# Moving every second PSUM evacuation of a linear-recurrence kernel from ScalarE to VectorE

## The chip, the cores and the metric

The kernel runs on all 8 cores of one Trainium2 chip. Each core computes one of the eight batch entries on its own, and no core waits for another. The time is the device time in microseconds (us) of the slowest core. Engine names are those of the profile: PE is TensorE (PEld its weight loads), DVE is VectorE, ACT is ScalarE, POOL is GpSimd, SP is SyncE. Times in ns are marked.

## What is computed

The input x has 8 batch entries of 8192 time steps with 1024 features. The reference, cut to what matters:

```python
lam = sigmoid(log_lambda_raw)
values = (1.0 - lam) * (x @ Wb.T + bb)
h = linear_recurrence(lam, values)        # h[t] = lam * h[t-1] + values[t]
z = layernorm(h @ Wc.T + bc + x) * gamma + beta
x = layernorm(x + z)
# int8 product: rows of x and columns of rhs scaled by their absolute maximum / 127 and rounded
q_x, s_x = quantise(x, per row);  q_r, s_r = quantise(rhs, per column)
x = layernorm(x + (q_x @ q_r) * s_x * s_r)
```

## The kernel before, in words

**Tiling.** A core walks its 8192 time steps in 32 chunks of 256 (CT). A chunk has two row blocks of 128 time steps (i = 0, 1), and the 1024 features are eight blocks of 128 (j = 0 to 7). Three products run on PE:
- mm1 (line 515, `mm1_group`): values, feature-major. For each j one group of 24 matmuls with 256 columns: eight each for high x high, low x high and high x low halves of a bf16 split. Group j goes to PSUM bank psm1[j % 2].
- mm2 (line 393, `mm2_group`): the product with Wc, four groups of 24 matmuls with 512 columns.
- mm3 (line 429, `mm3_group`): the quantised product, four groups of 8 matmuls with 512 columns, evacuated by ACT in line 438.

**Evacuation and scan.** `v_evac(c, j)` (line 527) takes group j out of PSUM and applies scale 1 - lam and a bias, per partition: one ACT instruction of 128x256. `scan_j(c, j)` (line 541) then runs the recurrence over these 256 time steps in place, on DVE. When all eight scans are done, `h_split` casts h to bf16 on ACT (line 552) and POOL computes the remainder (line 554). mm2 needs both.

**The rest of a chunk.** `p1a_i`, `p1b_i` and `p2_i` are the first two LayerNorms and the quantising, for row block i: squares with accumulation on ACT (568, 600), small statistics on DVE (462, 464, 472) and ACT (466, 469), normalising on ACT (580, 606), gamma, beta and the sum with x on DVE (584, 587, 591), the absolute maximum on DVE (610), scaling on ACT (619), rounding on DVE (622). `ln3a_i` (479) and `ln3b_i` (491) are the last LayerNorm, of the chunk before.

**Order of the work.** The program is written out in rounds k = 0 to 33. Round k holds transposes and mm1 of chunk k, mm2 and the first two LayerNorms of chunk k-1, and mm3 and the last LayerNorm of chunk k-2. Each engine executes its steps in program order. In the second half of a round the eight pairs of a group of mm1 and its evacuation are spread between the LayerNorm parts:

```python
mm1_pair(0); p1b_i(k-1, 0); mm1_pair(1); ln3a_i(k-2, 0); mm1_pair(2); p2_i(k-1, 0)
mm1_pair(3); ln3a_i(k-2, 1); mm1_pair(4); p1b_i(k-1, 1); mm1_pair(5); ln3b_i(k-2, 0), ln3b_i(k-2, 1)
mm1_pair(6); p2_i(k-1, 1); y_store; x_load; mm1_pair(7); scan_j(k, 7); h_split(k)
```

`mm1_pair(j)` records group j, evacuation j and, from j = 1, scan j-1, in this order.

**Who waits for whom.** `Planner.step` derives the waits from names of tiles that are read and written. All eight evacuations and scans of a chunk use one name, `vh0` or `vh1`. So scan j-1 also waits for evacuation j, which stands ahead of it, and evacuation j waits for scan j-2. Group j of mm1 waits for evacuation j-2, since it writes the same bank of psm1.

Of the kernel before, what the change touches and what calls it, by code (L numbers as in the profile page):

```python
# [7 lines left out]
AF = mybir.ActivationFunctionType  # L8
OP = mybir.AluOpType
# [108 lines left out]
def build_nc(T=8192, CT=256):  # L118
# [17 lines left out]
    with contextlib.ExitStack() as stk:  # L136
        E = stk.enter_context

        def sbt(name, shape, dt=F32):
            return E(nc.sbuf_tensor(name, shape, dt))  # L140
# [11 lines left out]
        omlc = sbt("omlc", [128, NDT])  # L152
        omlbb = sbt("omlbb", [128, NDT])
# [37 lines left out]
        vh = [big1[:, 4096:6144], big1[:, 6144:8192]]  # L191
# [10 lines left out]
        psm1 = [E(nc.psum_tensor(f"psm1{i}", [128, 512], F32)) for i in range(2)]  # L202
# [7 lines left out]
        for en in ("sync", "gpsimd"):  # L210
            for r in range(Planner.NDMA):
                sems[f"{en}_dma{r}"] = E(nc.semaphore(f"s_{en}_dma{r}"))

        P = Planner()
# [3 lines left out]
               writes=["iotaA"])  # L218
        P.step("gpsimd", lambda e: e.iota(iotaB[:], [[0, 128]], channel_multiplier=1,
                                          allow_small_or_imprecise_dtypes=True),  # L220
               writes=["iotaB"])
        P.step("vector", lambda e: e.tensor_tensor(idf[:], iotaA[:], iotaB[:], OP.is_equal),
               reads=["iotaA", "iotaB"], writes=["idf"])
# [6 lines left out]
               reads=["wSc"], writes=["wSc"])  # L230
        P.step("vector", lambda e: e.reciprocal(i127[:], i127[:]), reads=["i127"], writes=["i127"])
        P.step("vector", lambda e: e.tensor_scalar(wNc[:], wSc[:], -1.0, 1.0, OP.mult, OP.add),
               reads=["wSc"], writes=["wNc"])
        P.step("vector", lambda e: e.tensor_scalar(cxc[:], wSc[:], C52, C23, OP.mult, OP.bypass),
               reads=["wSc"], writes=["cxc"])
        P.step("vector", lambda e: e.scalar_tensor_tensor(cxc[:], wNc[:], C23, cxc[:], OP.mult, OP.add),
               reads=["wNc", "cxc"], writes=["cxc"])
# [15 lines left out]
               reads=["lamc"], writes=["lamc"])  # L253
        P.step("vector", lambda e: e.tensor_scalar(omlc[:], lamc[:], -1.0, -1.0,
                                                   OP.mult, OP.subtract),
               reads=["lamc"], writes=["omlc"])
        P.step("vector", lambda e: e.tensor_tensor(omlbb[:], omlc[:], bbcol[:], OP.mult),
               reads=["omlc", "bbcol"], writes=["omlbb"])
# [19 lines left out]
        for jj in range(NDT):  # L278
            bk = jj % 2
            for kk in range(NDT):  # L280
# [3 lines left out]
                    reads=["wst", "idf"], writes=[f"pstx{bk}"])  # L284
                if kk % 4 == 3:
# [3 lines left out]
                        reads=[f"pstx{bk}"], writes=[f"rtst{jj}"])  # L289
        for jj in range(NDT):  # L290
# [5 lines left out]
               reads=["csc", "i127"], writes=["csc"])  # L296
        P.step("vector", lambda e: e.tensor_copy(icsc[:], csc[:]), reads=["csc"], writes=["icsc"])
        P.step("vector", lambda e: e.reciprocal(icsc[:], icsc[:]), reads=["icsc"], writes=["icsc"])
        for jj in range(NDT):
# [3 lines left out]
                reads=[f"rtst{jj}", "icsc", "zcol"], writes=[f"rtst{jj}"])  # L303
            P.step("vector", lambda e, s=sl: e.tensor_scalar(
                rtst[:, s], rtst[:, s], cxc[:], cxc[:], OP.add, OP.subtract),
                reads=[f"rtst{jj}", "cxc"], writes=[f"rtst{jj}"])
            P.step("vector", lambda e, s=sl: e.tensor_scalar(
                qrsT[:, s], rtst[:, s], 127.0, -127.0, OP.min, OP.max),
                reads=[f"rtst{jj}"], writes=["qrsT"])
        for jj in range(NDT):  # L310
            for kk in range(NDT):
# [3 lines left out]
                    reads=["qrsT", "idb"], writes=["pstq"])  # L315
            P.step("scalar", lambda e, j=jj: e.copy(qrs[:, j * D:(j + 1) * D], pstq[:]),
                   reads=["pstq"], writes=["qrs"])
# [5 lines left out]
            reads=["csrowd"], writes=["csbc"], dma=True)  # L323
# [200 lines left out]
        def v_evac(c, j):  # L524
            p = c & 1
            bk = j % 2
            P.step("scalar", lambda e, jj=j, b=bk, pp=p: e.activation(  # L527
                vh[pp][:, jj * CT:(jj + 1) * CT], psm1[b][:, 0:CT], AF.Identity,
                bias=omlbb[:, jj:jj + 1], scale=omlc[:, jj:jj + 1]),
                reads=[f"psm1{bk}", "omlbb", "omlc"], writes=[f"vh{p}"])  # L530

        def scan_j(c, j):
            p = c & 1
# [92 lines left out]
        for k in range(NCH + 2):  # L626
# [27 lines left out]
            def mm1_pair(j):  # L654
                if k < NCH:
                    mm1_group(k, j)
                    v_evac(k, j)
                    if j >= 1:
                        scan_j(k, j - 1)
# [79 lines left out]
```

How the kernel before makes its waits and increments, by code:

```python
    def replay(self, eng_name, e, sems):  # L105
        for waits, fn, dma, tag in self.steps[eng_name]:
            for sem_name, val in waits:
                e.wait_ge(sems[sem_name], val)
            if isinstance(fn, list):
                for f in fn[:-1]:
                    f(e)
                ins = fn[-1](e)
            else:
                ins = fn(e)
            ins.then_inc(sems[tag[0]], 16 if dma else 1)
# [581 lines left out]
            @blk.gpsimd  # L697
            def _(e):
                P.replay("gpsimd", e, sems)
                for r in range(Planner.NDMA):
                    uses = (n_out_dma - 1 - r) // Planner.NDMA + 1 if r < n_out_dma else 0
                    if uses > 0:
                        e.wait_ge(sems[f"gpsimd_dma{r}"], 16 * uses)
```

## Time and profile before

| | |
|---|---|
| median of 3 runs | 2704.59 us (2702.23 to 2815.58) |
| the profiled execution | 2701.14 us |
| span of its slowest core, core 1 | 2699.6 us (the cores: 2694.2 to 2699.6) |
| mean granted clock of TensorE on core 1 | 0.876 of full speed |
| busy: PE, DVE, ACT, POOL | 71%, 36%, 40%, 17% of the span |
| evacuation, line 527 (ACT, 256 times) | 551 ns each |
| scan, line 541 (DVE, 256 times) | 746 ns each |

The span reaches from the first to the last instruction of a core, and 1.5 us of the profiled execution's time lie around it. Busy is the time in which an engine executes, so the rest of its span is waiting. A granted clock of 1.0 is 2.4 GHz and one of 0.5 is 1.2 GHz.

### The profile page before, as it was taken

How to read it: one execution, taken by the hardware profiler on the slowest of the kernel's cores; microseconds unless marked ns; L12 is line 12 of the kernel's file. 1: busy time of each engine (PE TensorE's matmuls, PEld its weight loads, DVE VectorE, ACT ScalarE, POOL GpSimd, SP SyncE). 2: the span in 40 equal slices, each digit the busy share in tenths (PEclk: the TensorE clock that was granted, in tenths of full speed). 3: DMA queues.
4: the chain of work that ended last, by engine and by line, in shares of the span. 5: the costliest groups of instructions: out<-in, count | busy, mean ns of one | idle time of the engine just before them, and what ended most of it. 6: DMA issues, size and time to landing. Idle time of an engine off the chain costs nothing.

```text
span 2699.6 us, 32538 instructions; the slowest of 8 cores (2694.2 to 2699.6 us)
## 1 busy us (share of the span) xinstructions
PE 1912.0 (71%) x11392; PEld 1193.4 (44%) x11392; DVE 961.4 (36%) x1962; ACT 1068.6 (40%) x1733; POOL 456.1 (17%) x200
## 2 busy tenths in 40 slices
PE   0348777777777777777877777778777777778761
PEld 0125444444454444444544444445444444445430
DVE  1223333344333334343333333433333333433332
ACT  2133344444343444444433344443334444434333
POOL 0001121211112221120212211211122121112220
PEclk9999988888998888888989888889888888899885
DMA  5110000111101010000000000000011110100000
GB/s 148 62 39 1 17 32 32 32 32 32 32 1 32 32 32 32 32 32 32 13 19 32 32 32 32 32 32 28 5 32 32 32 32 32 32 32 1 31 16 31
DMA packets 23376, 83.88 MB, mean 31 GB/s; under 512 B 3248, under 2 KB 3248, under 8 KB 23216
## 3 DMA queue, kind: packets, MB, share of 16 engines
q1 hardware_dynamic: 14336, 47.72, 6.5%
q0 software_dynamic: 8880, 34.08, 3.1%
q8 instruction: 93, 1.52, 0.2%
q14 instruction: 67, 0.55, 0.1%
HBM read 48.24 MB, written 33.56 MB: 30 GB/s over the span
## 4 chain that ended last, share of the span: by engine, by line
PE 40%; ACT 21%; DVE 19%; issue 13%; POOL 3%; DMA 2%; DVEq 1%; ACTq 0%; SPq 0%; POOLq 0%
PE psm L393 25%; PE psm L429 8%; DVE big L541 4%; ACT big L606 3%; ACT big L619 3%; DVE stats L610 3%; DVE big L587 3%; DVE big L584 3%; POOL Ab L446 3%; ACT big L580 3%; ACT big L600 2%; ACT big L527 2%; PE pstq L369 2%; PE pstx L350 2%; ACT stats L466 2%
## 5 line engine op out<-in xcount | busy, mean ns | idle before, releaser
L515 PE MATMUL psm<-big,wbh 128*128 128x256 bf16 x4096 | 565.6, 291 | 269.9 <-ACT big L527 267.6
L515 PEld LDWEIGHTS psm<-big,wbh 128*128 128x128 bf16 x4096 | 420.2, 104 | 371.7 <-issue 293.9
L393 PE MATMUL psm<-wch,big 128*128 128x512 bf16 x2048 | 504.0, 391 | 0.4 <-POOL big L554 0.3
L438 ACT ACTIVATE Ab<-psm,zcol,stats 128x512 f32<-128x512 f32 x128 | 99.0, 774 | 598.2 <-PE psm L429 594.0
L393 PEld LDWEIGHTS psm<-wch,big 128*128 128x128 bf16 x2048 | 205.6, 101 | 249.8 <-issue 27.1
L515 PE MATMUL psm<-big,wbl 128*128 128x256 bf16 x2048 | 303.9, 298 | 0.0
L446 POOL TENSOR_TENSOR Ab<-Ab,csbc 128x1024 f32<-128x1024 f32 x64 | 150.4, 2350 | 731.1 <-ACT Ab L438 731.1
L409 DVE SCALAR_TENSOR_TENSOR big<-psm,big 128x512 f32<-128x512 f32 x128 | 88.5, 692 | 484.6 <-PE psm L393 481.3
L429 PE MATMUL psm<-qrs,big 128*128 128x512 bf16 x1024 | 244.2, 382 | 6.0 <-ACT Ab L438 5.2
L393 PE MATMUL psm<-wcl,big 128*128 128x512 bf16 x1024 | 242.1, 379 | 0.0
L515 PEld LDWEIGHTS psm<-big,wbl 128*128 128x128 bf16 x2048 | 219.3, 107 | 42.9
L369 PE MATMUL pstq<-idb,big 128*128 128x128 bf16 x512 | 74.2, 298 | 216.2 <-DVE big L622 105.8
L350 PE MATMUL pstx<-idf,big 128*128 128x128 f32 x512 | 128.2, 401 | 131.5 <-DMA big<-x 124.7
L541 DVE TENSOR_TENSOR_SCAN big<-lamc,big 128x256 f32<-128x256 f32 x256 | 191.1, 746 | 68.1 <-ACT big L527 64.8
L554 POOL TENSOR_TENSOR big<-big 128x2048 bf16<-128x2048 f32 x32 | 129.9, 4059 | 464.3 <-ACT big L552 464.3
L450 DVE SCALAR_TENSOR_TENSOR Ab<-Ab,big 128x1024 f32<-128x1024 f32 x64 | 78.4, 1226 | 296.1 <-POOL Ab L446 296.1
L568 ACT ACTIVATE big<-big 128x1024 f32<-128x1024 f32 x64 | 67.6, 1057 | 271.4 <-DVE stats L566 271.4
L527 ACT ACTIVATE big<-psm,omlbb,omlc 128x256 f32<-128x256 f32 x256 | 141.2, 551 | 84.1 <-PE psm L515 61.6
L499 POOL DMA_DIRECT2D y<-big x32 | 24.4, 762 | 882.1 <-ACT big L491 567.9
L358 DVE TENSOR_TENSOR big<-pstx,big 128x512 bf16<-128x512 f32 x128 | 88.4, 691 | 206.8 <-ACT big L355 170.1
L369 PEld LDWEIGHTS pstq<-idb,big 128*128 128x128 bf16 x512 | 44.3, 126 | 260.6 <-issue 260.5
L429 PEld LDWEIGHTS psm<-qrs,big 128*128 128x128 bf16 x1024 | 100.3, 98 | 129.0 <-issue 10.1
(72 smaller groups left out, 1794.2 us busy)
## 6 DMA issues: line engine op xcount, KB each, us to landing
big<-x SPq DMA_DIRECT2D x32, 1024.0 KB, 6.4
y<-big POOLq DMA_DIRECT2D x32, 1024.0 KB, 8.0
big<-wbT SPq DMA_DIRECT2D x1, 4096.0 KB, 23.5
big<-wcT SPq DMA_DIRECT2D x1, 4096.0 KB, 16.5
big<-rhs SPq DMA_DIRECT2D x1, 4096.0 KB, 15.8
gbc<-gamma SPq DMA_DIRECT2D x1, 512.0 KB, 7.3
bbc<-beta SPq DMA_DIRECT2D x1, 512.0 KB, 8.3
ccbc<-bc SPq DMA_DIRECT2D x1, 512.0 KB, 11.1
```

The costliest lines, as they stand in the source:

```text
L350: items.append((lambda e, j=jj, i=ii, oo=o, b=bk, pp=p: e.transpose(pstx[b][:, oo * 128:(oo + 1) * 128], x_[pp][:, i * D + j * 128: i * D ...
L358: P.step("vector", lambda e, gg=g, b=bk, pp=p: e.tensor_tensor(xl[pp][:, 2 * gg * CT: 2 * (gg + 1) * CT], pstx[b][:, 0:512], xh[pp][:, 2 * ...
L369: items.append((lambda e, j=jj, i=ii, oo=o, pp=p: e.transpose(pstq[:, oo * 128:(oo + 1) * 128], q_[pp][:, i * D + j * 128: i * D + (j + 1) ...
L393: e.matmul(psm2[b][:, 0:512], hh[pp][:, kk * CT + ii * 128: kk * CT + (ii + 1) * 128], ww[:, kk * D + nn * 512: kk * D + (nn + 1) * 512], ...
L409: acc=sc("szn", i * 2 + n, 1): e.scalar_tensor_tensor(B_[pp][:, ii * D + nn * 512: ii * D + (nn + 1) * 512], psm2[b][:, 0:512], 1.0, A_[pp ...
L429: st=(k == 0), sp=(k == NDT - 1): e.matmul(psm3[:, 0:512], qT[pp][:, kk * CT + ii * 128: kk * CT + (ii + 1) * 128], qrs[:, kk * D + nn * 5 ...
L438: e.activation(Ab[:, ii * D + nn * 512: ii * D + (nn + 1) * 512], psm3[:, 0:512], AF.Identity, bias=zcol[:], scale=s),
L446: P.step("gpsimd", lambda e, ii=i: e.tensor_tensor(Ab[:, ii * D:(ii + 1) * D], Ab[:, ii * D:(ii + 1) * D], csbc[:], OP.mult), reads=["Ab", ...
L515: st=(idx == 0), sp=(idx == nmm - 1): e.matmul(psm1[b][:, 0:CT], w[:, kk * D + jj * 128: kk * D + (jj + 1) * 128], xx[pp][:, kk * CT:(kk + ...
L527: P.step("scalar", lambda e, jj=j, b=bk, pp=p: e.activation(vh[pp][:, jj * CT:(jj + 1) * CT], psm1[b][:, 0:CT], AF.Identity, bias=omlbb[:, ...
L541: P.step("vector", lambda e, jj=j, pp=p, ini=init: e.tensor_tensor_scan(vh[pp][:, jj * CT:(jj + 1) * CT], lamc[:, jj:jj + 1].broadcast_to( ...
L554: P.step("gpsimd", lambda e, pp=p: e.tensor_tensor(xl[pp][:], vh[pp][:], xh[pp][:], OP.subtract), reads=[vhk, xhk], writes=[xlk])
```

## The change

`v_evac` keeps its ACT instruction for even j. For odd j (1, 3, 5, 7) the same evacuation is a `tensor_scalar` on DVE, with the same scale and bias as two pointer scalars (one value per partition each). Names of tiles read and written stay the same, and so does the place in the program. All lines behind it have a number that is higher by 6, so the scan becomes line 547, line 591 becomes 597, line 622 becomes 628.

```diff
         def v_evac(c, j):
             p = c & 1
             bk = j % 2
-            P.step("scalar", lambda e, jj=j, b=bk, pp=p: e.activation(
-                vh[pp][:, jj * CT:(jj + 1) * CT], psm1[b][:, 0:CT], AF.Identity,
-                bias=omlbb[:, jj:jj + 1], scale=omlc[:, jj:jj + 1]),
-                reads=[f"psm1{bk}", "omlbb", "omlc"], writes=[f"vh{p}"])
+            if j % 2 == 0:
+                P.step("scalar", lambda e, jj=j, b=bk, pp=p: e.activation(
+                    vh[pp][:, jj * CT:(jj + 1) * CT], psm1[b][:, 0:CT], AF.Identity,
+                    bias=omlbb[:, jj:jj + 1], scale=omlc[:, jj:jj + 1]),
+                    reads=[f"psm1{bk}", "omlbb", "omlc"], writes=[f"vh{p}"])
+            else:
+                P.step("vector", lambda e, jj=j, b=bk, pp=p: e.tensor_scalar(
+                    vh[pp][:, jj * CT:(jj + 1) * CT], psm1[b][:, 0:CT],
+                    omlc[:, jj:jj + 1], omlbb[:, jj:jj + 1], OP.mult, OP.add),
+                    reads=[f"psm1{bk}", "omlbb", "omlc"], writes=[f"vh{p}"])
```

DVE's queue in a round of the middle, before, from the beta addition of row block 0 to the maximum of p2 (in these lists `big` stands for any of the large working tiles, `psm` for the PSUM banks of the products, and the scan is printed as SCALAR_TENSOR_TENSOR with lamc):

```order
L587 TENSOR_TENSOR big<-big,bbc 128x1024
L591 SCALAR_TENSOR_TENSOR big,stats<-big 128x1024
L541 SCALAR_TENSOR_TENSOR big<-lamc,big 128x256
L462 TENSOR_TENSOR stats<-stats 128x1
L464 SCALAR_TENSOR_TENSOR stats<-stats 128x1
L472 SCALAR_TENSOR_TENSOR stats<-stats 128x1
L541 SCALAR_TENSOR_TENSOR big<-lamc,big 128x256
```

The same stretch of DVE's queue in the changed kernel:

```order
L593 TENSOR_TENSOR big<-big,bbc 128x1024
L597 SCALAR_TENSOR_TENSOR big,stats<-big 128x1024
L533 TENSOR_SCALAR big<-psm,omlc,omlbb 128x256
L547 SCALAR_TENSOR_TENSOR big<-lamc,big 128x256
L462 TENSOR_TENSOR stats<-stats 128x1
L464 SCALAR_TENSOR_TENSOR stats<-stats 128x1
L472 SCALAR_TENSOR_TENSOR stats<-stats 128x1
L547 SCALAR_TENSOR_TENSOR big<-lamc,big 128x256
```

Evacuation 1 (line 533) stands between the sum with x and scan 0. Evacuation 5 stands in the same way behind the second line 597 of the round.

DVE's queue at the end of a round, before, from the reciprocal of row block 1 on (the rounding, the last two scans, the x transposes' remainders):

```order
L616 RECIPROCAL stats<-stats 128x1
L622 TENSOR_SCALAR big<-big,cxc 128x1024
L541 SCALAR_TENSOR_TENSOR big<-lamc,big 128x256 x2
L358 TENSOR_TENSOR big<-pstx,big 128x512 x4
L409 SCALAR_TENSOR_TENSOR big,stats<-psm,big 128x512 x2
```

The same in the changed kernel:

```order
L622 RECIPROCAL stats<-stats 128x1
L628 TENSOR_SCALAR big<-big,cxc 128x1024
L533 TENSOR_SCALAR big<-psm,omlc,omlbb 128x256
L547 SCALAR_TENSOR_TENSOR big<-lamc,big 128x256 x2
L358 TENSOR_TENSOR big<-pstx,big 128x512 x4
L409 SCALAR_TENSOR_TENSOR big,stats<-psm,big 128x512 x2
```

Evacuation 7 stands between the rounding and scans 6 and 7. Evacuation 3 stands behind the first rounding of the round, ahead of scan 2.

ACT's queue in the same round, before, from the scaling of row block 0 (line 619) to evacuation 6:

```order
L619 ACTIVATE big<-big,zcol,stats 128x1024
L527 ACTIVATE big<-psm,omlbb,omlc 128x256
L479 ACTIVATE big,stats<-Ab 128x1024
L466 ACTIVATE stats<-stats,epscol 128x1
L469 ACTIVATE stats<-stats 128x1
L527 ACTIVATE big<-psm,omlbb,omlc 128x256
L580 ACTIVATE big<-big,stats 128x1024
L527 ACTIVATE big<-psm,omlbb,omlc 128x256
L491 ACTIVATE big<-Ab,stats 128x1024 x2
L527 ACTIVATE big<-psm,omlbb,omlc 128x256
```

And in the changed kernel:

```order
L625 ACTIVATE big<-big,zcol,stats 128x1024
L479 ACTIVATE big,stats<-Ab 128x1024
L466 ACTIVATE stats<-stats,epscol 128x1
L469 ACTIVATE stats<-stats 128x1
L528 ACTIVATE big<-psm,omlbb,omlc 128x256
L586 ACTIVATE big<-big,stats 128x1024
L491 ACTIVATE big<-Ab,stats 128x1024 x2
L528 ACTIVATE big<-psm,omlbb,omlc 128x256
```

Evacuations 3 and 5 are gone from it, and 4 and 6 (line 528) remain. PE's queue is the same in both kernels.

## Rows read from the trace of the kernel before

**Rows 1.** The page, part 1: busy us, share of the span and instructions.

```profile
PE 1912.0 (71%) x11392; PEld 1193.4 (44%) x11392; DVE 961.4 (36%) x1962; ACT 1068.6 (40%) x1733; POOL 456.1 (17%) x200
```

**Rows 2.** The waits: engine, line, waited for, us in total, times, longest.

```profile
PE psm L515 <- ACT big L527: 267.6, 91, 5.2
```

**Rows 3.** The chain of waits, 1286 to 1372 us: start, us, what.

```profile
1345.51 0.68 DVE big L541
```

**Rows 4.** Timeline, place 1: start, us, engine, line, operation, count, idle before.

```profile
1327.61 0.08 DVE L591 DVE_READ_ACCUMULATOR big<-big 128x1 f32 x1
1327.61 0.74 DVE L541 TENSOR_TENSOR_SCAN big<-lamc,big 128x256 f32<-128x256 f32 x1
1328.27 0.13 DVE L462 TENSOR_TENSOR stats<-stats 128x1 f32<-128x1 f32 x1
1328.76 0.29 ACT L466 ACTIVATE stats<-stats,epscol 128x1 f32<-128x1 f32 x1 [3.57 <-DVE stats L464]
```

**Rows 5.** Timeline, place 3.

```profile
1337.14 0.54 ACT L527 ACTIVATE big<-psm,omlbb,omlc 128x256 f32<-128x256 f32 x1
1337.34 0.81 DVE L622 TENSOR_SCALAR big<-big,cxc 128x1024 bf16<-128x1024 f32 x1 [1.44 <-ACT big L619]
1337.59 1.04 ACT L479 ACTIVATE big<-Ab 128x1024 f32<-128x1024 f32 x1
...
1337.94 1.87 PE L515 MATMUL psm<-big,wbh 128*128 128x256 bf16 x8 [5.10 <-ACT big L527]
1338.07 0.75 DVE L541 TENSOR_TENSOR_SCAN big<-lamc,big 128x256 f32<-128x256 f32 x1
1338.54 0.19 ACT L479 ACTIVATION_READ_ACCUMULATOR big<-Ab 128x1 f32 x1
1338.83 0.16 DVE L462 TENSOR_TENSOR stats<-stats 128x1 f32<-128x1 f32 x1
```

**Rows 6.** Timeline, place 5: in the round before, and in this one.

```profile
1269.00 0.75 DVE L541 TENSOR_TENSOR_SCAN big<-lamc,big 128x256 f32<-128x256 f32 x1
...
1269.87 0.55 ACT L527 ACTIVATE big<-psm,omlbb,omlc 128x256 f32<-128x256 f32 x1
...
1343.24 2.56 ACT L491 ACTIVATE big<-Ab,stats 128x1024 f32<-128x1024 f32 x2
...
1345.43 0.08 DVE L591 DVE_READ_ACCUMULATOR big<-big 128x1 f32 x1
1345.43 0.75 DVE L541 TENSOR_TENSOR_SCAN big<-lamc,big 128x256 f32<-128x256 f32 x1
...
1346.27 0.56 ACT L527 ACTIVATE big<-psm,omlbb,omlc 128x256 f32<-128x256 f32 x1 [0.47 <-DVE big L541]
```

**Rows 7.** Timeline, place 7.

```profile
1353.90 0.55 ACT L527 ACTIVATE big<-psm,omlbb,omlc 128x256 f32<-128x256 f32 x1
1354.10 0.81 DVE L622 TENSOR_SCALAR big<-big,cxc 128x1024 bf16<-128x1024 f32 x1 [1.44 <-ACT big L619]
1354.83 1.60 DVE L541 TENSOR_TENSOR_SCAN big<-lamc,big 128x256 f32<-128x256 f32 x2
```

**Rows 8.** Groups of instructions by form: busy us, mean ns, idle before.

```profile
L527 ACT ACTIVATE big<-psm,omlbb,omlc 128x256 f32<-128x256 f32 x256 | 141.2, 551 | 84.1 <-PE psm L515 61.6 <-DVE big L541 17.8 <-DVE big L584 4.1
...
L409 DVE SCALAR_TENSOR_TENSOR big<-psm,big 128x512 f32<-128x512 f32 x128 | 88.5, 692 | 484.6 <-PE psm L393 481.3
...
L591 DVE SCALAR_TENSOR_TENSOR big<-big 128x1024 f32<-128x1024 f32 x64 | 78.4, 1225 | 7.0 <-DVE big L587 0.5
...
L304 DVE TENSOR_SCALAR big<-big,cxc 128x1024 f32<-128x1024 f32 x8 | 6.5, 807 | 1.4 <-ACT big L301 1.4
L307 DVE TENSOR_SCALAR big<-big 128x1024 bf16<-128x1024 f32 x8 | 5.5, 694 | 0.9
```

**Rows 9.** Timeline, PE in groups 5 to 7 of mm1, the round before.

```profile
1261.51 1.87 PE L515 MATMUL psm<-big,wbh 128*128 128x256 bf16 x8 [4.82 <-ACT big L527]
...
1263.17 1.91 PE L515 MATMUL psm<-big,wbl 128*128 128x256 bf16 x8
...
1268.43 1.91 PE L515 MATMUL psm<-big,wbh 128*128 128x256 bf16 x16
```

## The prediction

> **What bounds the kernel now.** I read the page first, then the waits, then the chain of work that ended last, and last the timeline of one round. On the page the reader sees that no engine is full: PE is busy 1912.0 us of 2699.6, DVE 961.4, ACT 1068.6 [rows 1]. Busy time therefore says nothing about who sets the end, and "ACT has more work than DVE, so move some over" is not an argument by itself. In the waits PE stands idle before a group of line 515 (the first product, mm1) for 267.6 us in 91 waits, each ended by an ACT instruction of line 527 [rows 2]. That invites a second error, that the evacuation of line 527 is slow. It takes 0.55 us [rows 8]. PE waits because line 527 stands in ACT's queue behind other work, and that work is a ping-pong between ACT and DVE: LayerNorm statistics, normalising, quantising, for two row blocks in turn.
>
> The chain shows which pieces count. In this half of a round it runs through the scans of line 541 on DVE [rows 3], and the timeline shows why at four places of a round:
> - Place 1, between lines 591 and 462: the scan starts as line 591's accumulator is read (1327.61), line 462 starts 0.66 later, and ACT, idle for 3.57 us, goes on with line 466 once line 464 is done [rows 4]. ACT has slack here, DVE none.
> - Place 3, behind the quantising of line 622: the scan starts 0.73 after line 622 and ends at 1338.82. ACT's line 479 ends with its accumulator at 1338.73, and line 462 starts at 1338.83 [rows 5]. Both sides arrive nearly together.
> - Place 5, behind the second line 591: scan 4 starts at 1345.43, and evacuation 6 on ACT starts 0.84 later, because the planner makes it wait for that scan. ACT had been idle for 0.47 us [rows 6]. One round earlier the distance is 0.87, with ACT just free (1269.00 to 1269.87), so in both rounds the scan is as late as anything.
> - Place 7, behind the second line 622: scans 6 and 7 start at 1354.83 and take 1.60; evacuation 7 on ACT (1353.90, 0.55 long) was over by 1354.45 [rows 7]. The cast of line 552, the rest of h_split, PE's transposes and the second product (mm2) all follow from scan 7.
>
> So from the first line 591 to the end of the round the path runs through DVE at exactly the four places where the odd evacuations will now stand. None of the four odd line 527s is on that path today.
>
> **The change part by part.** *Removed from ACT:* four evacuations a round, each 0.45 us from its start to the next instruction's (1337.14 to 1337.59 [rows 5]). Number 1 goes where ACT waits 3.57 us afterwards, so it is worth nothing. Number 3 goes ahead of line 479, which then ends 0.45 earlier, but line 462 also waits for the scan, so it is worth at most the 0.09 us between 1338.74 and 1338.83 (1338.74 is where line 462 would start 0.08 before the scan's end, as it does at place 1 [rows 4]). Number 5 stands ahead of the two line 491s (1343.24 plus 2.56, [rows 6]), after which ACT idles for the scan, worth nothing. Number 7 is hidden behind line 622, worth nothing. Together: 0.09 us a round.
>
> *Added on DVE:* four tensor_scalars from PSUM, 128x256 fp32, with two pointer scalars. No row of before shows this one, so I bound it. Line 409 is a DVE pass over 512 elements of PSUM in 692 ns, line 591 one over 1024 elements in 1225, so an element costs 533/512 = 1.04 ns, and 256 elements come to 692 - 266 = 426 ns [rows 8]. Two pointer scalars cost 807 - 694 = 113 ns, from the tensor_scalar with cxc twice (line 304) against the one with constants (line 307) [rows 8]. Sum: 0.54 us. Lines 304 and 307 do 1024 elements at half the price of an element. If that held from PSUM too, line 304's 807 less 768 elements at 0.52 gives 0.41 us, the low end. The high end is 0.75, the longest DVE pass of this size (the scan). I take 0.54, as line 409 is the row with the same source.
>
> On this the Trainium skill (VectorE: DVE Perf Modes, section "Why PSUM operands drop a tier") says that an fp32 operand in PSUM holds VectorE to one element a cycle. No row of a tensor_scalar from PSUM can confirm it here. By that rule the item is the 0.54; without it, 0.41. The same page (section on the TRN2 errata) gives 120 cycles plus the elements for VectorE from PSUM, an estimate of 376/0.96 = 392 ns; by it the sum below would be 4 x 0.49 - 0.09 = 1.87, times 31 = 58, and the time 2759. Line 409's 692 ns is above what that formula gives for 512 elements, 658, so here the trace says the page is low.
>
> Each added instruction also gets a gap behind it: the scan must wait for its result on the same engine, and two scans that do so take 1.60 for 2 x 0.75, a gap of 0.10 [rows 7]. So one place costs 0.64 us. In front there is no new gap, since the evacuation waits only for PE and for evacuations that are done, and can start where the scan starts now.
>
> *Along the path:* place 1 delays lines 462, 464 and ACT's 466 by 0.64. Place 3 delays line 462 by another 0.64 - 0.09. Place 5 delays scan 4 and thereby evacuation 6 and line 600 by 0.64. Place 7 delays scans 6 and 7 and the cast by 0.64. Queued behind each on DVE stands the statistics or scan chain, and ACT waits for exactly that. A round gets 4 x 0.64 - 0.09 = 2.47 us longer. Rounds k=1 to 31 have this shape (k=0 has no LayerNorm part, and its evacuations lie beside mm1; the last two have no mm1). 31 x 2.47 = 76.6 us.
>
> *PE:* bank 1 of psm1 now comes free when DVE gets there. PE starts 0.26 after an evacuation's end (1337.14 + 0.54, then 1337.94 [rows 5]). Group 3 of mm1 waits until 1327.61 + 0.54 + 0.26 = 1328.4. It is followed by group 4 and then by an idle PE anyway, so it costs nothing. Group 5 now follows evacuation 3 on DVE, at 1338.07 + 0.64 + 0.54 + 0.26 = 1339.5 instead of 1337.94 [rows 5], 1.57 later. Evacuation 6 needs group 6. In the round before, groups 5 and 6 ran from 1261.51 until about 1269.3 (the last eight of group 6 are the first half of the sixteen matmuls at 1268.43) [rows 9], 7.8 us; 1.57 later that is 1270.9. DVE allows evacuation 6 at 1269.87 + 3 x 0.64 - 0.09 = 1271.7. Covered by 0.8 us; if the cover goes, see the rival on PE. The x load is issued behind line 597, about 1.2 us later, and its transposes are not needed until the cast of h_split, which moves by more.
>
> *Sum:* the profiled execution took 2701.1 us, 3.5 below the median of 2704.6 of the runs. 2701.1 + 76.6 = 2777.7, that is 2778. With the low end of 0.41 us: 4 x 0.51 - 0.09 = 1.95, times 31 = 60, 2761. With the high end of 0.75: 3.31 x 31 = 103, 2804. A measurement of this kernel tells about 2% from no change, here 2759.
>
> **Rivals.**
> *Only half of the places count* (12%). If at place 3 the true last arrival is ACT's accumulator (1338.73 is within 0.1 us of the scan) and at place 5 it is ACT's own queue (as at 1269.87), ACT's relief of 0.45 pays back most of it. Then only places 1 and 7 cost: 1.28 x 31 = 40, 2741. Against it: at both places DVE was as late already, and there is no slack to take up 0.64.
> *ACT sets the round, and the change is a gain* (5%), the one that ends at not slower. This holds if the scans of places 1, 3, 5 and 7 had idle time of more than 0.64 ahead of their consumers; then the evacuations ahead of lines 479 and 491 leave the path, 2 x 0.45 x 31 = 28, 2673. It decides at place 3, by whether the scan's end was over 0.64 earlier than line 479's. For it speaks that ACT has 107 us more work than DVE [rows 1]; against it the times in rows 5 and 6.
> *PE becomes late* (8%). The half clock shows in group 5: eight matmuls take 1.66 us (1261.51 to 1263.17 [rows 9]), 0.21 each, the 1.2 GHz level, after PE had stood idle. If groups 5 and 6 both run so, that is 48 x 0.21 = 10.0 us instead of 7.8. Evacuation 6 comes at 1263.07 + 10.0 + 0.2 = 1273.3 instead of 1271.7, 1.6 more a round, 50 us in all, 2828. For it speaks that PE gets one more wait a round; against it that the clock was back before group 6 in that round although PE had stood still for almost 5 us. [...]
>
> **How the numbers follow.** The forecast, 2761 to 2804 with 2778 as its centre, has 70%, the rivals 12, 5 and 8, and 5% stay for the clock's phase at the start of mm2 and what I don't see. The range goes down to 2740, which takes in half of the first rival, and up to 2805. Outside lie the second rival, half of the first, most of the third. Slower by over 2%: 66 of the forecast's 70 (the rest is its cheap end), 8 of PE late, 4 of the remainder, 78%. Within 2%: 4, 12, 3 and 1, 20%. Faster by over 2%: 2%, if ACT's relief counted at all four places (56 us).
>
> **What would show it.** In the profile after: the new DVE group at about 540 ns, 128 times, DVE busy up by about 69 us and ACT busy down by about 70; scan 0 starting 0.64 after the accumulator read of line 597; evacuation 6 at 1.48 instead of 0.84 behind that read; ACT still idle ahead of line 466, by 0.64 plus 0.45 more; a new wait of PE for DVE ahead of groups 3, 5 and 7; the distance of one h_split cast to the next up by 2.5 us, and the mm2 stage unchanged. The forecast is wrong if line 462 at place 3 waits for ACT's line 479, if evacuation 6 waits for PE, or if the DVE evacuation takes under 0.4 us.

## The result, and the profile after

The changed kernel takes 2771.13 us, the kernel before 2703.59 us (medians of 8 runs each). The ratio of the two is 1.0251, with a 95% interval of 1.0240 to 1.0263, so the change makes the kernel 2.5% slower. The forecast was 2778, with a range of 2740 to 2805. In some executions of most kernels here the cores of one die show a lower granted clock and take longer (2815.58 us in one of the 8 before), and no comparison in this document uses them.

The profiled execution of the changed kernel took 2773.26 us. Its eight cores span from 2752.5 to 2771.7 us, while before they lay between 2694.2 and 2699.6. The page of the slowest, core 5, part 1 (answering to [rows 1]):

```profile
PE 1933.5 (70%) x11392; PEld 1203.9 (43%) x11392; DVE 1028.5 (37%) x2090; ACT 1010.4 (36%) x1605; POOL 456.0 (16%) x200
```

DVE has 67 us more work and ACT 58 us less. The forecast for ACT was 70, which counts the 0.55 us of each evacuation; an evacuation overlaps the next instruction on ACT, and 128 times the 0.45 us from its start to the next start are 58. By busy time the two engines are now balanced, and the kernel is slower. The reader should keep this row as the example of what busy time doesn't say.

The group of the new instruction, and the evacuation that stayed on ACT (by form: busy us, mean ns, idle before; answering to [rows 8]):

```profile
L528 ACT ACTIVATE big<-psm,omlbb,omlc 128x256 f32<-128x256 f32 x128 | 71.1, 555 | 123.3 <-DVE big L547 96.8 <-PE psm L515 26.4 <-issue 0.2
L533 DVE TENSOR_SCALAR big<-psm,omlc,omlbb 128x256 f32<-128x256 f32 x128 | 69.2, 541 | 12.3 <-PE psm L515 12.3
```

The new instruction takes 541 ns, not less than the 551 of the one it replaced. The waits (answering to [rows 2]):

```profile
ACT stats L466 <- DVE stats L464: 274.5, 191, 5.0
...
PE psm L515 <- DVE big L533: 221.8, 76, 5.8
...
ACT big L528 <- DVE big L547: 96.8, 32, 5.8
...
PE psm L515 <- ACT big L528: 83.9, 30, 3.1
```

PE's wait ahead of mm1 is now 221.8 + 83.9 = 305.7 us instead of 267.6. Most of it has changed its name, from ACT to DVE, and the whole has grown (core 5 here, core 1 there).

The timeline of core 5 at place 1, between the first sum with x and the statistics of ln3a (answering to [rows 4]):

```profile
1201.73 0.08 DVE L597 DVE_READ_ACCUMULATOR big<-big 128x1 f32 x1
1201.73 0.54 DVE L533 TENSOR_SCALAR big<-psm,omlc,omlbb 128x256 f32<-128x256 f32 x1
1202.37 0.75 DVE L547 TENSOR_TENSOR_SCAN big<-lamc,big 128x256 f32<-128x256 f32 x1
...
1203.04 0.13 DVE L462 TENSOR_TENSOR stats<-stats 128x1 f32<-128x1 f32 x1
...
1203.53 0.30 ACT L466 ACTIVATE stats<-stats,epscol 128x1 f32<-128x1 f32 x1 [4.67 <-DVE stats L464]
```

The scan starts 0.64 behind the accumulator read, where it used to start with it, and line 462 follows 1.31 behind it instead of 0.66. ACT idles 4.67 us instead of 3.57: the 0.64 by which DVE is later, and the 0.45 that ACT no longer spends on evacuation 1. ACT's relief has become ACT's idle time.

Place 3, behind the first rounding (answering to [rows 5]):

```profile
1212.03 1.04 ACT L479 ACTIVATE big<-Ab 128x1024 f32<-128x1024 f32 x1
1212.23 0.81 DVE L628 TENSOR_SCALAR big<-big,cxc 128x1024 bf16<-128x1024 f32 x1 [1.44 <-ACT big L625]
1212.96 0.54 DVE L533 TENSOR_SCALAR big<-psm,omlc,omlbb 128x256 f32<-128x256 f32 x1
1212.98 0.19 ACT L479 ACTIVATION_READ_ACCUMULATOR big<-Ab 128x1 f32 x1
1213.60 0.75 DVE L547 TENSOR_TENSOR_SCAN big<-lamc,big 128x256 f32<-128x256 f32 x1
1213.64 1.87 PE L515 MATMUL psm<-big,wbh 128*128 128x256 bf16 x8 [4.38 <-DVE big L533]
1214.27 0.13 DVE L462 TENSOR_TENSOR stats<-stats 128x1 f32<-128x1 f32 x1
```

ACT's line 479 is now done at 1213.17, over one microsecond ahead of line 462, which waits for the scan alone. PE starts group 5 at 1213.64, 0.14 after the end of evacuation 3.

Place 5, behind the second sum with x (answering to [rows 6]). Evacuation 6 on ACT starts 1.50 behind the accumulator read instead of 0.84, after 2.93 us of idle time. In all of the rounds 2 to 31 of this core it waits for the scan:

```profile
1220.85 0.08 DVE L597 DVE_READ_ACCUMULATOR big<-big 128x1 f32 x1
1220.85 0.54 DVE L533 TENSOR_SCALAR big<-psm,omlc,omlbb 128x256 f32<-128x256 f32 x1
...
1221.50 0.75 DVE L547 TENSOR_TENSOR_SCAN big<-lamc,big 128x256 f32<-128x256 f32 x1
1222.35 0.57 ACT L528 ACTIVATE big<-psm,omlbb,omlc 128x256 f32<-128x256 f32 x1 [2.93 <-DVE big L547]
```

The chain of work that ended last, in the same round, names evacuations on DVE as pieces of its own, at places 1, 3, 5 and 7 (start, us, what). Before, none of the odd ones was in it:

```profile
1201.81 0.47 DVE big L533
...
1212.96 0.55 DVE big L533
...
1220.94 0.47 DVE big L533
...
1230.91 0.55 DVE big L533
```

To see the whole kernel and not one round, I cut each of the rounds 2 to 31 of two cores at five marks of the timeline (starts of the first and second sum with x, of the first and second rounding, and of the cast of h) and took the median of each stretch, in us:

| stretch | before, core 0 | after, core 0 | after, core 5 | core 0 | forecast |
|---|---|---|---|---|---|
| first sum to first rounding (place 1) | 10.62 | 11.26 | 11.28 | +0.64 | +0.64 |
| first rounding to second sum (place 3) | 6.94 | 7.47 | 7.48 | +0.53 | +0.55 |
| second sum to second rounding (place 5) | 9.82 | 10.47 | 10.49 | +0.65 | +0.64 |
| second rounding to cast (place 7) | 2.42 | 3.07 | 3.06 | +0.65 | +0.64 |
| sum | 29.80 | 32.27 | 32.31 | +2.47 | +2.47 |

The rest of a round, from the cast over mm2 to the first sum with x, was forecast as unchanged. It isn't. Its mean over these 30 rounds falls from 46.76 to 46.22 us on core 0 and from 46.86 to 46.52 on core 5.

### The profile page after: what moved, and what is told of

Same layout as the page of the kernel before. It is cut to its first block, busy times and chain, and to the rows that moved or that the text cites. A ratio compares the mean times of both kernels' runs of the same rounds, so it can differ in the third digit from the quotient of the medians.

```text
span 2771.7 us, 32539 instructions; the slowest of 8 cores (2752.5 to 2771.7 us)
## 1 busy us (share of the span) xinstructions
PE 1933.5 (70%) x11392; PEld 1203.9 (43%) x11392; DVE 1028.5 (37%) x2090; ACT 1010.4 (36%) x1605; POOL 456.0 (16%) x200
## 4 chain that ended last, share of the span: by engine, by line
PE 39%; ACT 21%; DVE 19%; issue 15%; POOL 3%; DMA 2%; DVEq 1%; ACTq 0%; SPq 0%; POOLq 0%
PE psm L393 24%; PE psm L429 8%; ACT big L612 3%; ACT big L625 3%; DVE stats L616 3%; POOL Ab L446 3%; ACT big L586 3%; DVE big L593 3%; DVE big L590 3%; DVE big L547 3%; ACT big L606 2%; DVE big L533 2%; ACT big L528 2%; PE pstq L369 2%; PE pstx L350 2%
## 5 line engine op out<-in xcount | busy, mean ns | idle before, releaser
L515 PE MATMUL psm<-big,wbh 128*128 128x256 bf16 x4096 | 585.9, 297 | 307.9 <-DVE big L533 221.8
L515 PEld LDWEIGHTS psm<-big,wbh 128*128 128x128 bf16 x4096 | 426.8, 106 | 420.7 <-issue 335.4
L393 PE MATMUL psm<-wch,big 128*128 128x512 bf16 x2048 | 497.5, 387 | 0.4 <-POOL big L560 0.3
L515 PE MATMUL psm<-big,wbl 128*128 128x256 bf16 x2048 | 313.0, 304 | 0.0
L515 PEld LDWEIGHTS psm<-big,wbl 128*128 128x128 bf16 x2048 | 225.2, 110 | 48.2
L466 ACT ACTIVATE stats<-stats,epscol 128x1 f32<-128x1 f32 x192 | 57.1, 297 | 274.5 <-DVE stats L464 274.5
```

The costliest lines, as they stand in the source:

```text
L393: e.matmul(psm2[b][:, 0:512], hh[pp][:, kk * CT + ii * 128: kk * CT + (ii + 1) * 128], ww[:, kk * D + nn * 512: kk * D + (nn + 1) * 512], ...
L515: st=(idx == 0), sp=(idx == nmm - 1): e.matmul(psm1[b][:, 0:CT], w[:, kk * D + jj * 128: kk * D + (jj + 1) * 128], xx[pp][:, kk * CT:(kk + ...
```

## The experiments

### Single places

`only5` and `only7` move one evacuation each, all others stay on ACT.

```diff
-            if j % 2 == 0:
+            if j != 5:
```

> Only evacuation 5 on DVE, 1, 3 and 7 on ACT as before. Place theory (a DVE instruction put on the DVE part of the path costs its length and a gap): the stretch from the second sum with x to the second rounding grows by 0.65 us a round (9.82 to 10.47), the three other stretches stay, 31 x 0.65 = 20 us, ratio near 1.007, moved by up to 15 us by the clock at the start of mm2. Rival 'only half of the places count' (at place 5 ACT's own queue is the last arrival and its relief pays back): that stretch grows by 0.2 or less, 0 to 6 us.

> Only evacuation 7 on DVE, 1, 3 and 5 on ACT as before. Place theory: only the stretch from the second rounding to the cast of h grows, 2.42 to 3.07, 31 x 0.65 = 20 us, ratio near 1.007, moved by the clock. Rival: the cost is a matter of DVE's load, in which case all four stretches grow by a quarter of what the whole change gave each (0.16).

Measured: `only5` 1.0093 of the kernel before (95% interval 1.0050 to 1.0136), `only7` 1.0071 (1.0032 to 1.0111). Both intervals hold the 1.007 that was expected, and neither is narrow enough to give the price of one place, so the stretches decide. The stretches on core 0, medians: `only5` 10.62, 6.94, **10.47**, 2.42; `only7` 10.62, 6.94, 9.82, **3.06**. Place 5 of `only5`, on core 0:

```profile
1276.35 0.08 DVE L597 DVE_READ_ACCUMULATOR big<-big 128x1 f32 x1
1276.35 0.54 DVE L533 TENSOR_SCALAR big<-psm,omlc,omlbb 128x256 f32<-128x256 f32 x1
...
1276.99 0.75 DVE L547 TENSOR_TENSOR_SCAN big<-lamc,big 128x256 f32<-128x256 f32 x1
1277.84 0.56 ACT L528 ACTIVATE big<-psm,omlbb,omlc 128x256 f32<-128x256 f32 x1 [2.94 <-DVE big L547]
```

Each of the two evacuations costs 0.65 us a round in its own stretch and nothing in the other three. That refutes both rivals: the load theory would have spread the cost, and at place 5 ACT's relief pays nothing back. Each price is also the growth of the same stretch in the whole change, where the other three evacuations had moved as well. Evacuations 1 and 3 were not moved alone.

### ACT's relief taken back

`act_dummy` is the changed kernel plus an ACT instruction of the same size, on constant data into a scratch tile, at each place that an evacuation left.

```diff
+                P.step("scalar", lambda e, jj=j: e.activation(
+                    junk[:, 0:CT], ccbc[:, 0:CT], AF.Identity,
+                    bias=omlbb[:, jj:jj + 1], scale=omlc[:, jj:jj + 1]),
+                    reads=["ccbc", "omlbb", "omlc"], writes=["junk"])
```

> The changed kernel, and in addition an ACT instruction of the same size (128x256, from a constant tile into a scratch tile) at each place where an evacuation left ACT's queue, so ACT's relief is taken back and DVE's load stays. The added instruction is no part of the computation. Place theory: ACT's relief was worth nothing, so the four stretches stay within 0.05 us of the changed kernel's (11.26, 7.46, 10.47, 3.07) and the time within 0.5% of its 2771. Rival 'ACT's relief pays back part of the cost': 2 x 0.45 x 31 = 28 us more, 2799.

Measured: 2765.8 and 2776.6 us in two runs, on either side of 2771 and too few for an interval, so the rounds must decide. Their stretches on core 0 are 11.26, 7.46, 10.47 and 3.06, those of the changed kernel to 0.01, and the profiled cores span 2751.8 to 2775.0 us against its 2752.5 to 2771.7. Place 3 on core 5, with the added instruction in line 537 and the scan in line 551:

```profile
1288.65 0.58 ACT L537 ACTIVATE junk<-ccbc,omlbb,omlc 128x256 f32<-128x256 f32 x1
...
1290.08 0.19 ACT L479 ACTIVATION_READ_ACCUMULATOR big<-Ab 128x1 f32 x1
1290.22 0.75 DVE L551 TENSOR_TENSOR_SCAN big<-lamc,big 128x256 f32<-128x256 f32 x1
1290.89 0.13 DVE L462 TENSOR_TENSOR stats<-stats 128x1 f32<-128x1 f32 x1
...
1291.38 0.29 ACT L466 ACTIVATE stats<-stats,epscol 128x1 f32<-128x1 f32 x1 [1.11 <-DVE stats L464]
```

The only thing that moved is ACT's idle time, 1.11 us instead of 1.60 ahead of line 466. What the change took from ACT was worth nothing at all four places. That holds for place 3 too, whose stretch grows by 0.53 and not by 0.64: with the added instruction ACT's line 479 ends at 1290.27, still 0.62 ahead of line 462, and the stretch stays at 7.46. The missing 0.1 us is time that DVE had to spare there before, when line 462 waited for ACT.

### The shared names

`names` is the kernel before with a name for each block of `vh`, so the planner sets only waits that the data need. `names_dve` is the same edit on the changed kernel.

```diff
-                reads=[f"psm1{bk}", "omlbb", "omlc"], writes=[f"vh{p}"])
+                reads=[f"psm1{bk}", "omlbb", "omlc"], writes=[f"vh{p}{j}"])
...
-            vhk = f"vh{p}"
+            vhk = f"vh{p}{j}"
...
-            vhk = f"vh{p}"
+            vhk = [f"vh{p}{j}" for j in range(NDT)]
```

> The kernel before with all evacuations on ACT, but each of the eight blocks of vh has its own name in the planner, so that scan j-1 no longer waits for evacuation j and evacuation j no longer for scan j-2. Place theory: only place 5 gains, where evacuation 6 waited for scan 4 up to 0.47 us: the stretch from the second sum to the second rounding falls from 9.82 by 0 to 0.47, 0 to 15 us in all, ratio 0.995 to 1.0. Rival 'the shared names are what puts evacuation and scan on the path': about 0.5 us at each of four places, 60 us less, ratio 0.978.

> The changed kernel (odd evacuations on DVE) with a name of its own for each block of vh, as in the run 'names'. Place theory: against 'names' (10.62, 6.94, 8.96, 2.20 in the four stretches) places 1, 3 and 7 still cost, about 0.54 each since the scan behind the evacuation no longer waits for it (places 3 a little less), and place 5 costs nothing, since evacuation 6 on ACT no longer waits for scan 4: 11.1, 7.4, 9.0, 2.75, together 1.5 us a round. Rival 'the shared names made the DVE evacuation dear': all four stretches stay within 0.1 of those of 'names'.

Measured: `names` 0.9806 of the kernel before (0.9750 to 0.9862), faster, though not clearly by 2%; `names_dve` 1.0054 (1.0036 to 1.0071). The profiled execution of `names` spans 2656.4 us on its slowest core against 2699.6 before, 1.6% less. Stretches on core 5: `names` 10.62, 6.94, 8.96, 2.20; `names_dve` 11.07, 7.27, 9.47, 2.66. Place 5 of `names`, core 5:

```profile
1325.98 2.56 ACT L491 ACTIVATE big<-Ab,stats 128x1024 f32<-128x1024 f32 x2
...
1328.45 0.55 ACT L527 ACTIVATE big<-psm,omlbb,omlc 128x256 f32<-128x256 f32 x1
1328.46 0.08 DVE L591 DVE_READ_ACCUMULATOR big<-big 128x1 f32 x1
1328.46 1.39 DVE L541 TENSOR_TENSOR_SCAN big<-lamc,big 128x256 f32<-128x256 f32 x2
...
1328.90 1.05 ACT L600 ACTIVATE big<-big 128x1024 f32<-128x1024 f32 x1
```

Evacuation 6 now starts with the accumulator read and not 0.84 after it, and line 600 follows 0.44 behind that read. The place was named rightly, places 1 and 3 gained nothing, and so far this is the place theory. But both sizes were missed. The stretch fell by 0.86, not by 0.47 at most, for line 491 also started earlier than I had assumed (1.33 ahead of the second sum against 1.04). At place 7 the stretch fell by 0.22, which I had not forecast: two scans that don't wait for each other take 1.39 instead of 1.60 us. The ratio is near the one the rival named, yet not by its mechanism, which needed about 0.5 at each of four places. Averaged over 30 rounds of core 5 the four stretches fall by 0.97 us, which makes 29 us, and the part from the cast to the first sum falls from 46.86 to 46.29, another 17. The second part is the clock of the next section: 3 slow starts of mm2 instead of 15.

In `names_dve` the DVE evacuations cost, against `names`, 0.45 and 0.33 at places 1 and 3 and 0.46 at place 7, a little under the 0.54 of the instruction. So the rival falls: waits by name are not what makes the evacuation dear. At place 5, where I expected nothing, the cost is 0.51. The view of the waits on core 5 and the timeline of one round give the cause, `names_dve`:

```profile
ACT big L528 <- PE psm L515: 89.1, 36, 6.5
...
1345.49 1.86 PE L515 MATMUL psm<-big,wbh 128*128 128x256 bf16 x8 [3.57 <-DVE big L533]
...
1352.47 0.56 ACT L528 ACTIVATE big<-psm,omlbb,omlc 128x256 f32<-128x256 f32 x1 [1.41 <-PE psm L515]
```

In `names` this wait was 61.4 us in 41 times, and there all eight evacuations were on ACT. In `names_dve` the even ones alone wait 89.1: once evacuation 6 no longer waits for the scan it waits for group 6, which is late, because group 5 had to wait for evacuation 3 on DVE. Evacuation 6 waits for PE in all of the rounds 2 to 31, and in `names` in none of them. How late PE is goes along with its clock. In 10 of the 30 rounds the stretch is 9.01 us, 0.05 above the 8.96 of `names`, so there the expectation held, and the mean granted clock between evacuations 3 and 6 was 0.77 to 0.80. In the other 20 it is 9.24 to 10.64 us, at 0.64 to 0.78. That is the prediction's third rival, PE being late, in a kernel in which its cover of 0.8 us is gone.

### The clock at the start of mm2

The part of the round that got shorter holds mm2. PE's first eight matmuls of mm2 in three rounds running, kernel before, core 1:

```profile
1209.56 3.19 PE L393 MATMUL psm<-wch,big 128*128 128x512 bf16 x8
...
1286.75 2.15 PE L393 MATMUL psm<-wch,big 128*128 128x512 bf16 x8
...
1363.16 3.19 PE L393 MATMUL psm<-wch,big 128*128 128x512 bf16 x8
```

And of the changed kernel, core 4:

```profile
1310.01 1.89 PE L393 MATMUL psm<-wch,big 128*128 128x512 bf16 x8
...
1388.49 1.89 PE L393 MATMUL psm<-wch,big 128*128 128x512 bf16 x8
...
1466.96 1.89 PE L393 MATMUL psm<-wch,big 128*128 128x512 bf16 x8
```

Eight take 1.89 us at a granted clock of 1.00 (2.4 GHz), as in the last three rows, and 3.19 at a mean of 0.59, as in the first and the third. In both kernels PE does transposes before that, at 0.50 (1.2 GHz): before, 4.6 us of matmuls in the 9.5 us up to 1209.5. What differs is when the clock rises. In rounds 3 to 9 before, on core 1, that is in turn 2.0 to 2.4 us and 0.0 to 0.2 us behind the first matmul of mm2; after, on core 4, it is between 0.6 ahead and 0.7 behind in 16 of the rounds 2 to 19, and later in two. I call a start slow if the eight take over 2.3 us. In the rounds 2 to 31 there are 14 slow starts before on core 0 and 15 on core 5. After, it is 2 on core 0, none on core 1, 2 on core 4, 6 on core 7 and 9 on core 5. The stage itself has not changed. On core 5 the part from the cast to the first sum takes 46.10 us before and 46.15 after in rounds whose eight take at most 2.0 us, and 47.39 and 47.20 in rounds with a slow start. So the changed kernel loses less time to the clock, and cores lose differently, which is most of the 19 us by which their spans now differ: between core 6 and core 5 the 30 rounds make 14 us. The other 5 come ahead of the first cast, whose start differed between cores before as well (211.4 to 219.4 us). `pad7` adds one DVE instruction, on constant data, to ask whether the length of the round decides this.

```diff
+                if j == 7:
+                    P.step("vector", lambda e: e.tensor_tensor(
+                        junk[:, 0:512], ccbc[:, 0:512], csbc[:, 0:512], OP.add),
+                        reads=["ccbc", "csbc"], writes=["junk"])
```

> The changed kernel and one more DVE instruction ahead of evacuation 7 (128x512 from two constant tiles into a scratch tile, no part of the computation). Place theory: the stretch from the second rounding to the cast grows by 0.61 to 0.79 from 3.07, the others stay: 20 to 24 us. Clock theory (mm2's first matmuls are at half clock in about every second round of the kernel before and in hardly any of the changed kernel because the length of the round decides it): at 79.2 us a round they are at half clock again in a third to a half of the rounds, their eight take 2.5 us or more instead of 1.9, and the stretch from the start of mm2 to the last line 450 gets 0.3 to 0.6 longer: 30 to 42 us together, about 2805. Rival (the new waits ahead of mm2 keep the clock up): they stay at 1.9, 2793.

Measured: 2793.7 us, 1.0323 of the kernel before (1.0297 to 1.0349). Only the stretch of place 7 grew, 3.07 to 3.67. The first eight are slow in 9 rounds on core 0 and 12 on core 5, against 2 and 9. The die medians of the span went from 2757.1 and 2759.8 to 2786.0 and 2787.6, 28 to 29 us, of which 0.60 x 31 = 18.6 are the instruction. So slow starts did come back, as the clock theory said. But the whole time rose by 22.6 us, by which the rival's 2793 was right and my 2805 wrong: a whole time is that of the slowest core, and that core had 9 slow starts already. Length alone is not the rule either. `only5` and `only7`, at 77.3 to 77.5 us a round (medians), have 19 and 20 slow starts, each on both cores, `names_dve` at 77.3 only 9 on core 0 and 10 on core 5. That the clock gives back part of the cost is shown. What decides in which round stays open.

### The same instructions, in idle time

If place is all that counts, evacuations and scans should cost nothing where their engine waits anyway. `slots_act` has all evacuations on ACT, `slots_dve` the odd ones on DVE. Both have a name for each block of `vh`, as `names` has, and both record evacuations and scans in the idle times that the profile shows (core of `slots_act`, with `hook`, `slot_a` and `slot_b` called behind lines 464, 606 and 616):

```diff
+            def slot_a0():
+                ev(3); sn(2); mm(5); ev(4); mm(6)
+            def slot_b0():
+                sn(3)
+            def slot_a1():
+                ev(7); sn(6)
+            def slot_b1():
+                sn(7)
...
-            mm1_pair(1)
+            mm(1); ev(1); mm(2); mm(3)
             if 2 <= k:
-                ln3a_i(k - 2, 0)
+                ln3a_i(k - 2, 0, lambda: sn(0))
...
-                p2_i(k - 1, 0)
+                p2_i(k - 1, 0, slot_a0, slot_b0)
```

> All evacuations on ACT, own names, and evacuations and scans recorded where their engine is idle: evacuations 3, 4 and 7 behind the normalising of line 606, scans 0 and 4 behind line 464, scans 2 and 6 ahead of the maximum, 3 and 7 behind the reciprocal, 1 and 5 in the shadow of the squares. Place theory: place 1 gains 0.6, place 3 0.45, place 5 0.9, place 7 2.6 us a round (the cast then follows the scaling on ACT at once): 4.5 x 31 = 140 us less than before, 2560, moved by up to 20 by the clock. Rival (PE's product mm1 sets the round once the scans are out of the way): no stretch gains more than 'names' gave, 2655.

> The odd evacuations on DVE as in the changed kernel, but recorded like the scans where DVE is idle (1 behind line 464, 3 ahead of the first maximum, 5 behind the second sum, 7 behind the second reciprocal). Place theory: a DVE evacuation costs nothing where DVE waits anyway, so the time is within 1.5% of 'slots_act' and far below both kernels, 2560 to 2610. Rival 'an evacuation on DVE costs its length wherever it stands': 4 x 0.6 x 31 = 74 us above 'slots_act'.

Measured: `slots_act` 2539.64 us, 0.9381 of the kernel before (0.9356 to 0.9407), 6.2% faster. `slots_dve` took 2566.8 and 2567.5 us in two runs, too few for an interval, and its profiled execution's slowest core spans 2566.0 us against 2537.1 of `slots_act`, 1.1% more. The stretches on core 0, medians (in both kernels the cast starts ahead of the second rounding, so the last stretch is negative):

| stretch | before | slots_act | slots_dve |
|---|---|---|---|
| first sum to first rounding | 10.62 | 9.97 | 10.88 |
| first rounding to second sum | 6.94 | 6.03 | 6.04 |
| second sum to second rounding | 9.82 | 8.70 | 8.71 |
| second rounding to cast | 2.42 | -0.20 | -0.01 |
| sum | 29.80 | 24.51 | 25.61 |

The whole gain of `slots_act` is 5.29 us a round instead of the 4.5 expected: 0.65 and 2.62 at places 1 and 7 as expected, 0.91 and 1.12 at places 3 and 5 instead of 0.45 and 0.9. The names alone had given 0.86 and 0.22 of it, at places 5 and 7. Place 7 of `slots_act`, where the scan is line 543, the scaling 623, the rounding 626 and the cast 554:

```profile
1273.70 0.74 DVE L543 TENSOR_TENSOR_SCAN big<-lamc,big 128x256 f32<-128x256 f32 x1
...
1275.02 0.54 ACT L529 ACTIVATE big<-psm,omlbb,omlc 128x256 f32<-128x256 f32 x1
...
1277.03 0.75 DVE L543 TENSOR_TENSOR_SCAN big<-lamc,big 128x256 f32<-128x256 f32 x1
1277.19 1.24 ACT L623 ACTIVATE big<-big,zcol,stats 128x1024 f32<-128x1024 f32 x1 [1.62 <-DVE stats L619]
1278.33 1.88 ACT L554 CAST big<-big 128x2048 bf16<-128x2048 f32 x1
```

The cast follows the scaling at once, instead of waiting for the rounding and two scans. The rival that PE would set the round at 2655 is refuted.

Against `slots_act` the DVE evacuations cost 1.10 us a round, less than half of the 2.47 they cost in the changed kernel, and the rival's 74 us, which would be 2614, is too dear. The stretches show which of them cost. Evacuation 5 costs 0.01. Evacuation 7 costs 0.19: scan 7 now ends together with ACT's scaling (at 1356.59 and 1356.58 in one round), and the cast starts 0.10 behind it, where in `slots_act` it starts 0.10 ahead of the scaling's end. The other 0.91 lies in the first stretch, where evacuations 1 and 3 stand. One round of it on core 0, with the evacuation in line 535:

```profile
1333.33 1.87 PE L517 MATMUL psm<-big,wbh 128*128 128x256 bf16 x8 [3.08 <-DVE big L535]
...
1337.55 0.54 DVE L535 TENSOR_SCALAR big<-psm,omlc,omlbb 128x256 f32<-128x256 f32 x1 [1.21 <-PE psm L517]
```

Group 3 of mm1 waits for evacuation 1, which in its pause comes late, and evacuation 3 then waits for group 3, ahead of the maximum that the round needs. In 24 of the rounds 2 to 31 evacuation 3 waits 0.88 to 2.39 us for PE, at a mean granted clock of 0.50 to 0.68 from shortly before group 3 to evacuation 3, and the stretch is 10.77 to 12.43 us. In the other six the clock was 0.95 to 1.00, evacuation 3 doesn't wait, and the stretch is 9.97, that of `slots_act`. So the time of DVE in a pause costs nothing, as the place theory says. What it had left out is that a later evacuation also gives PE its bank later. Why the clock was up in those six rounds stays open.

## Why the prediction was right

The direction, the range and the mechanism held, and one term, the unchanged rest of a round, was wrong. Point by point:

- *The odd evacuations will stand on DVE's part of the path, at four places.* Right at each: four stretches grow, the chain names the four instructions, and those of places 5 and 7 have the same price alone (`only5`, `only7`).
- *The instruction takes 0.54 us.* 541 ns. It was worked out as one element in 1.04 ns, with the fixed part of line 409 and 113 ns for two pointer scalars. At half the price of an element it would have been 0.41. The Trainium skill's rule (VectorE: DVE Perf Modes, "Why PSUM operands drop a tier"), that an fp32 operand in PSUM holds VectorE to one element a cycle, agrees with the 541. The 392 ns that the prediction estimated from the same page's table for PSUM sources is too low.
- *A gap of 0.10 ahead of the dependent scan, 0.64 a place.* Right: 1201.73 to 1202.37.
- *ACT's relief is worth 0.09 us a round.* The 0.09 is right as a term, and the four stretches grew by the 2.47 of the sum, but it was put down to the wrong side. `act_dummy` takes the relief back and no stretch changes, so the relief is worth nothing. The 0.09 is what the scan of place 3 had to spare while line 462 waited for ACT.
- *PE is covered by 0.8 us.* Right for the changed kernel as far as evacuation 6 goes: it waits for the scan in all of the rounds 2 to 31. Group 5 started 0.14 behind the end of evacuation 3, not 0.26, and the size of the cover was not measured. In `names_dve`, whose evacuation 6 is no longer held by the scan, the late group 6 is the wait in all of them.
- *31 x 2.47 = 76.6 us, with the mm2 stage unchanged.* The unchanged stage is the term that was off. On core 0 the four stretches did give 2.48 (means), but the part from the cast to the first sum fell by 0.54 a round. 30 rounds of 1.93 and 2.6 in round 1 make 60.5, and the span grew by 58.9. On core 5, the slowest, 30 rounds of 2.19 and 3.8 in round 1 make 69.5; another 7.6 came ahead of the first cast, where the first cast starts at 219.0 instead of 211.4, a part that the edit hardly touches. Before, the eight cores' first casts lay between 211.4 and 219.4, so this is a difference between executions, and it happened to bring the time nearer to the forecast. The medians of the whole kernel differ by 67.5. I had put the clock's phase into the remainder with 5%, without a size or a sign. It was worth 10 us on core 5 and 16 on core 0, and it was a gain. Even so the range would have held: core 0 alone would have given about 2756.
- *The rivals.* Half of the places (2741), ACT sets the round (2673) and PE late (2828) did not happen. The first named places 3 and 5 as cheap. At place 5 the cost is full, 0.65, and at place 3 it is 0.53, which `act_dummy` leaves as it is.

## What to carry to other kernels

Before you move work to the less busy engine, find where it will stand in that engine's queue, and whether somebody waits for what is queued behind it. Here two engines play ping-pong, each idle over half of the time, and an instruction of 0.54 us costs 0.65 if it is put between the ball and the bat. In the pause it costs nothing as long as it fits and no third engine waits for its result. Moving evacuations and scans into the pauses, with a name for each block and without changing a single instruction's engine, brought 6.2% (names alone about 1.6 to 1.9%), where moving every second evacuation to the other engine lost 2.5%.

## What the runs showed of the hardware that was not expected

- The clock that mm2 finds depends on timing in a way that a local edit upsets. In the kernel before about every second round starts mm2 slowly, at a granted clock of 0.50 (14 of 30 on core 0; on core 5 such a round takes 1.3 us longer from the cast to the first sum). With 2 us more a round it is 2 of 30, with one more DVE instruction 9 again (all core 0). The same kernel can differ between cores: `slots_act` has 2 slow starts on core 0 and 24 on core 5, with rounds of 71.2 and 71.5 us.
- Two scans in a row take 1.60 us if the second waits for the first and 1.39 if it doesn't, so the wait for the own engine's result costs 0.21 here, of which I had counted only 0.10.
